# Vision tower on one Trainium2 core: quantization of q, k and v in four passes inside the scale chain, and embedding chunks in one transfer each

## The reference

```python
def fq_act(x, bits=8):                        # one scale for the whole tensor
    mn, mx = jnp.min(x), jnp.max(x)
    qmax = 2.0 ** bits - 1.0
    scale = jnp.maximum((mx - mn) / qmax, 1e-08)
    zero = jnp.round(-mn / scale)
    q = jnp.clip(ste_round(x / scale) + zero, 0.0, qmax)
    return ((q - zero) * scale, scale)
...
qkv = jnp.einsum('bnc,oc->bno', x, fq_weight(w_qkv)) + b_qkv
qkv, _ = fq_act(qkv)                          # first quantization, all three
q, _ = fq_act(qkv[:, :, :C])                  # second quantization, each its own
k, _ = fq_act(qkv[:, :, C:2 * C])
v, _ = fq_act(qkv[:, :, 2 * C:])
...
attn, kv_scale = fq_act(q @ k^T / 4)          # 12 heads of 16 features
out = int_softmax(attn, kv_scale) @ v
```

## Time and profile before

| | us |
|---|---|
| median of 3 runs | 379.75 |
| lowest, highest | 379.64, 383.16 |
| the profiled execution | 379.25 |
| its span in the profile | 377.4 |
| busy: PE, DVE, ACT, POOL | 291.3, 268.6, 203.1, 23.6 |

### The profile page before, as it was taken

One profiled execution on the slowest core, in us unless ns is written; L12 is line 12 of the kernel. 1 busy time (PEld: TensorE's weight loads), 2 busy tenths in 40 slices (PEclk: granted clock), 3 DMA queues, 4 the chain that ended last, 5 costly groups with the idle time before them and its releaser, 6 DMA issues.

```text
span 377.4 us, 5949 instructions
## 1 busy us (share of the span) xinstructions
PE 291.3 (77%) x2232; PEld 266.6 (71%) x2232; DVE 268.6 (71%) x714; ACT 203.1 (54%) x486; POOL 23.6 (6%) x46
## 2 busy tenths in 40 slices
PE   5789979989999999999881042079631598999991
PEld 4577968889999999999771022058420588999991
DVE  1069173888888888798668997975368648888851
ACT  0034546677777777877271467570010667777750
POOL 8010000000000000000000005800000000000000
PEclk9999996999999999999996555569555579999997
DMA  7960400253153132000000000000500013543401
GB/s 235 261 267 1 148 0 4 85 176 125 50 177 116 61 146 72 29 1 2 0 3 0 0 1 2 0 0 2 195 0 1 0 24 114 162 160 126 113 0 43
DMA packets 11548, 27.36 MB, mean 72 GB/s; under 512 B 1496, under 2 KB 3144, under 8 KB 11520
## 3 DMA queue, kind: packets, MB, share of 16 engines
q1 hardware_dynamic: 10944, 26.03, 21.2%
q0 software_dynamic: 576, 0.96, 1.0%
HBM read 26.54 MB, written 0.45 MB: 72 GB/s over the span
## 4 chain that ended last, share of the span: by engine, by line
PE 62%; DVE 22%; ACT 7%; DMA 3%; issue 2%; SPq 2%; DVEq 0%; ACTq 0%
PE bank L585 26%; PE bank L647 9%; PE bank L569 7%; PE bank L632 4%; PE bank L630 4%; DMA embed_area<-w_tok_dram 3%; PE bank L847 2%; DVE embed_area L1510 1%; PE bank L552 1%; PE bank L832 1%; ACT hid_hi L982 1%; DVE bn L1187 1%; PE bank L844 1%; DVE stat_q L1395 1%; PE bank L857 1%
## 5 line engine op out<-in xcount | busy, mean ns | idle before, releaser
L585 PE MATMUL bank<-hid_hi,pj_parts 128*128 128x260 f32 x288 | 76.2, 286 | 1.7 <-DVE hid_lo L1282 1.7
L982 ACT ACTIVATE hid_hi<-hidden_area 128x260 fp32r<-128x260 f32 x144 | 55.9, 422 | 38.8 <-DVE hidden_area L1277 37.6
L1282 DVE TENSOR_TENSOR hid_lo<-hidden_area,hid_hi 128x260 fp32r<-128x260 f32 x144 | 56.6, 427 | 9.9 <-ACT hid_hi L982 0.3
L585 PEld LDWEIGHTS bank<-hid_hi,pj_parts 128*128 128x128 f32 x288 | 54.1, 188 | 2.5 <-DVE hid_lo L1282 2.0
L975 ACT ACTIVATE hidden_area<-bank 128x260 f32<-128x260 f32 x144 | 49.1, 377 | 6.9 <-PE bank L632 6.1
L585 PE MATMUL bank<-xt_hi,fc_hi 128*128 128x260 f32 x144 | 42.8, 297 | 1.3 <-ACT hidden_area L973 1.3
L632 PE MATMUL bank<-xt_lo,fc_lo 128*128 128x260 f32 x144 | 42.2, 293 | 0.0
L585 PE MATMUL bank<-xt_lo,fc_hi 128*128 128x260 f32 x144 | 41.5, 288 | 0.0
L630 PE MATMUL bank<-xt_lo,fc_hi 128*128 128x260 f32 x144 | 41.5, 288 | 0.0
L585 PE MATMUL bank<-xt_hi,fc_lo 128*128 128x260 f32 x144 | 41.3, 287 | 0.0
L647 PE MATMUL bank<-hid_hi,pj_parts 128*128 128x260 f32 x144 | 40.8, 283 | 0.0
(11 more groups left out here) (297 smaller groups left out, 559.3 us busy)
## 6 DMA issues: line engine op xcount, KB each, us to landing
raw_area<-fc_dram SPq DMA_DIRECT2D x8, 768.0 KB, 4.3
raw_area<-pj_dram SPq DMA_DIRECT2D x8, 576.0 KB, 5.4
xn<-comb_dram SPq DMA_DIRECT2D x12, 260.0 KB, 3.3
raw_area<-fc_dram SPq DMA_DIRECT2D x6, 512.0 KB, 4.0
hidden_area<-comb_dram SPq DMA_DIRECT2D x9, 260.0 KB, 3.3
raw_area<-pj_dram SPq DMA_DIRECT2D x6, 384.0 KB, 4.4
embed_area<-patches_dram SPq DMA_DIRECT2D x8, 256.0 KB, 4.7
embed_area<-w_tok_dram SPq DMA_DIRECT2D x8, 96.0 KB, 7.6
```

What stands on the lines that cost most here:

```text
L585: mm = pe.matmul(out, lhs[a], rhs[b], start=start and n == 0, stop=stop and n == 2, skip_group_check=True)
L982: act.activation(hid_hi[:, x % 3, tok], hid_w[:, x % 2, tok], ACT.Copy).then_inc(hid_hi_ready[y], 1)
L1282: dve.tensor_tensor(hid_lo[:, x % 3, tok], hid_w[:, x % 2, tok], hid_hi[:, x % 3, tok].bitcast(F32), ALU.subtract).then_inc(hid_lo_ready[y ...
```

## The change

1. `patches` and `w_tok` become one tensor `embed_in` (in DRAM too), and each of the eight chunks is one transfer of 128 rows of 2816 bytes. PE waits for 16 in place of 32.
2. POOL waits for the last embedding chunk before it issues `wq_raw`; everything behind it on POOL's queue waits as well.
3. The two quantizations of q and of k are each two passes in place of three and a share of a joint one: (x * scale + MAGIC), then (x - MAGIC, min bound). The lower bound is left out, and so are the second lower bound `s2_lo` and `ext_q`. The passes of the first quantization are issued between the small instructions of the scale chain, as soon as `s1_inv` is known. v: ACT does scale and MAGIC of the first quantization after the new semaphore `s1_ready`, DVE clips, ACT multiplies by `ratio`, and DVE (behind `k_heads`) adds MAGIC and clips into `qkv_int`.
4. Two of the six `k_heads` copies (heads 4 and 5) are made by ACT after `k_int_ready`; PE waits for both sets.
5. On PE the wait for all nine groups of scores now stands ahead of `turn_v` in place of behind it.

```diff
-        patches = embed_area.take(128, [TOKK, B * PATCH])
-        w_tok = embed_area.take(128, [TOKK, D])
+        embed_in = embed_area.take(128, [TOKK, B * PATCH + D])
+        patches, w_tok = embed_in[:, :, 0:B * PATCH], embed_in[:, :, B * PATCH:]
...
+        K_HEADS_ACT = (4, 5)
...
             for k in range(TOKK):
-                sp.dma_start(patches[:, k, :], t["patches"][k]).then_inc(tok_in[k], 16)
-                sp.dma_start(w_tok[:, k, :], t["w_tok"][k]).then_inc(tok_in[k], 16)
+                sp.dma_start(embed_in[:, k, :], t["embed_in"][k]).then_inc(tok_in[k], 16)
...
             pool.dma_start(fold[:], t["fold"]).then_inc(consts_in, 16)
+            pool.wait_ge(tok_in[TOKK - 1], 16)
             pool.dma_start(wq_raw[:, 0:6, :], t["w_qkv"]).then_inc(wq_in, 16)
...
             for k in range(TOKK):
-                pe.wait_ge(tok_in[k], 32)
+                pe.wait_ge(tok_in[k], 16)
...
-            pe.wait_ge(k_heads_ready, 1)
+            pe.wait_ge(k_heads_ready, HC - len(K_HEADS_ACT))
+            pe.wait_ge(k_heads_act, len(K_HEADS_ACT))
...
+            pe.wait_ge(sc_ready, 9)
             turn_v()
-            pe.wait_ge(sc_ready, 9)
             statistics(1, stat_s[:], 2, 128)
...
             v = qkv[:, 4:6]
+            act.wait_ge(s1_ready, 1)
+            act.activation(v, v, ACT.Copy, scale=colp("s1_inv", DC)).then_inc(v_act, 1)
+            act.wait_ge(v_act, 1)
+            act.activation(v, v, ACT.Copy, bias=MAGIC).then_inc(v_act, 1)
+            act.wait_ge(v_dve, 1)
             act.wait_ge(s2_ready, 1)
-            act.activation(v, v, ACT.Copy, scale=colp("s1_inv", DC)).then_inc(v_act, 1)
-            act.wait_ge(v_dve, 1)
-            act.activation(v, v, ACT.Copy, bias=MAGIC).then_inc(v_act, 1)
-            act.wait_ge(v_act, 2)
-            act.activation(v, v, ACT.Copy, bias=-MAGIC).then_inc(v_act, 1)
-            act.wait_ge(v_act, 3)
             act.activation(v, v, ACT.Copy, scale=colp("ratio", DC, 2)).then_inc(v_act, 1)
+            act.wait_ge(k_int_ready, 1)
+            for head in K_HEADS_ACT:
+                act.activation(k_heads[:, :, :, head, :], qkv_int[:, 2:4], ACT.Copy,
+                               scale=head_mask[:, head:head + 1]).then_inc(k_heads_act, 1)
...
-            act.wait_ge(v_dve, 2)
-            act.activation(v, v, ACT.Copy, bias=MAGIC).then_inc(v_act, 1)
-            act.wait_ge(v_act, 5)
-            act.activation(qkv_int[:, 4:6], v, ACT.Copy, bias=-MAGIC).then_inc(v_int_ready, 1)
...
             scale_of("s1", col("gmax"), col("gneg"))
-            zero_of("s1", col("gneg"), col("s1_inv"))
...
+            def scaled(x, inv):
+                return step(dve.tensor_scalar(x, x, inv, MAGIC, ALU.mult, ALU.add))
+
+            def clipped(out, x, top):
+                return dve.tensor_scalar(out, x, MAGIC, top, ALU.subtract, ALU.min)
+
+            dve.tensor_scalar(col("s1_z"), col("gneg"), col("s1_inv"), MAGIC, ALU.mult, ALU.add).then_inc(s1_ready, 1)
+            exts = step(dve.tensor_scalar(ext_t[:], ext[:], col("s1_inv"), MAGIC, ALU.mult, ALU.add))
+            q_scaled = scaled(qq, colp("s1_inv", DC))
+            dve.wait_ge(s1_ready, 1)
+            step(dve.tensor_scalar(col("s1_hi"), col("s1_z"), -1.0, MAGIC + QMAX, ALU.mult, ALU.add))
+            step(dve.tensor_scalar(col("s1_lo"), col("s1_z"), MAGIC + QMAX, None, ALU.subtract))
+            tops = step(dve.tensor_scalar(col("s1_step"), col("s1"), 1.0 / QMAX, None, ALU.mult))
+            k_scaled = scaled(kk, colp("s1_inv", DC))
+            after(tops)
+            step(dve.tensor_scalar(ext_c[:, 0:3], ext_t[:, 0:3], MAGIC, col("s1_hi"), ALU.subtract, ALU.min))
+            exts = step(dve.tensor_scalar(ext_c[:, 3:6], ext_t[:, 3:6], MAGIC, col("s1_lo"), ALU.subtract, ALU.max))
+            q_clipped = step(clipped(qq, qq, colp("s1_hi", DC)))
+            after(exts)
+            ranges = step(dve.tensor_tensor(s2, ext_c[:, 0:3], ext_c[:, 3:6], ALU.add))
+            after(k_scaled)
+            k_clipped = step(clipped(kk, kk, colp("s1_hi", DC)))
+            after(ranges)
+            scales = step(dve.tensor_scalar(s2, s2, col("s1_step"), SMIN, ALU.mult, ALU.max))
+            dve.wait_ge(v_act, 2)
+            clipped(v, v, colp("s1_hi", DC)).then_inc(v_dve, 1)
+            after(scales)
             then(dve.reciprocal(s2i, s2))
...
+            dve.tensor_scalar(col("ratio"), s2i, col("s1"), None, ALU.mult).then_inc(s2_ready, 1)
             dve.wait_ge(s2_ready, 1)
...
+            zeros_at = step(dve.tensor_tensor(col("s2_z"), ext_c[:, 3:6], col("ratio"), ALU.mult))
+            q_scaled = scaled(qq, colp("ratio", DC, 0))
+            after(zeros_at)
+            zeros_at = step(dve.tensor_scalar(col("s2_z"), col("s2_z"), MAGIC, None, ALU.add))
+            k_scaled = scaled(kk, colp("ratio", DC, 1))
+            after(zeros_at)
+            then(dve.tensor_scalar(col("s2_hi"), col("s2_z"), -1.0, MAGIC + QMAX, ALU.mult, ALU.add))
+            q_int = step(clipped(qkv_int[:, 0:2], qq, colp("s2_hi", DC, 0)))
+            after(k_scaled)
+            clipped(qkv_int[:, 2:4], kk, colp("s2_hi", DC, 1)).then_inc(k_int_ready, 1)
+            after(q_int)
...
             for head in range(HC):
...
+                if head not in K_HEADS_ACT:
+                    dve.tensor_scalar(k_heads[:, :, :, head, :], qkv_int[:, 2:4], head_mask[:, head:head + 1], None,
+                                      ALU.mult).then_inc(k_heads_ready, 1)
+            dve.wait_ge(v_act, 3)
+            added = step(dve.tensor_scalar(v, v, MAGIC, None, ALU.add))
+            after(added)
+            clipped(qkv_int[:, 4:6], v, colp("s2_hi", DC, 2)).then_inc(v_int_ready, 1)
```

More of the change, by code:

```diff
@@ L202, in build @@
         ext_c = sb("ext_c", [128, 6])
-        ext_q = sb("ext_q", [128, 6])
         c = sb("consts", [128, 80])
@@ L216, in colp @@
             return c[0:p, at + i:at + i + 1]
-        for name in ("s1", "s1_inv", "s1_z", "s1_lo", "s1_hi", "gmax", "gneg", "qk", "alpha", "sa", "sa_inv", "sa_z", "sa_lo",
+        for name in ("s1", "s1_inv", "s1_z", "s1_lo", "s1_hi", "s1_step", "gmax", "gneg", "qk", "alpha", "sa", "sa_inv", "sa_z", "sa_lo",
                      "sa_hi", "x0", "neg_x0", "neg_inv_x0", "neg_x0_30", "quot_bias", "half_b", "sq_bias", "half_b2", "poly_c", "so", "so_inv", "so_z", "so_lo", "so_hi", "alpha_o", "omax",
@@ L293, in build @@
         stat_b = sem("stat_b")
+        s1_ready = sem("s1_ready")
         s2_ready = sem("s2_ready")
+        k_int_ready = sem("k_int_ready")
+        k_heads_act = sem("k_heads_act")
         v_act = sem("v_act")
@@ L1311, in statistics, with step, after @@
                 return PB[7][:, 0:n]
+            def step(ins):
+                steps[0] += 1
+                ins.then_inc(dve_done, 1)
+                return steps[0]
+            def after(n):
+                dve.wait_ge(dve_done, n)
             def scale_of(name, top, negmin, factor=None):
@@ L1414, in _ @@
-            then(dve.tensor_tensor(s2, ext_q[:, 0:3], ext_q[:, 3:6], ALU.subtract))
-            then(dve.tensor_scalar(s2, s2, 1.0 / QMAX, SMIN, ALU.mult, ALU.max))
-            then(dve.reciprocal(s2i, s2))
-            settle(dve.tensor_scalar(col("ratio"), s2i, col("s1"), None, ALU.mult))
-            then(dve.tensor_tensor(col("s2_z"), ext_q[:, 3:6], s2i, ALU.mult))
-            then(dve.tensor_scalar(col("s2_z"), col("s2_z"), -1.0, MAGIC, ALU.mult, ALU.add))
-            then(dve.tensor_scalar(col("s2_lo"), col("s2_z"), MAGIC, -1.0, ALU.subtract, ALU.mult))
@@ L1421, in _ @@
-            dve.tensor_scalar(col("s2_hi"), col("s2_z"), -1.0, MAGIC + QMAX, ALU.mult, ALU.add).then_inc(s2_ready, 1)
-            dve.wait_ge(s2_ready, 1)
-            z = qkv[:, 0:4]
-            then(dve.tensor_scalar(z, z, colp("s1_inv", DC), colp("s1_lo", DC), ALU.mult, ALU.max))
-            then(dve.tensor_scalar(z, z, colp("s1_hi", DC), MAGIC, ALU.min, ALU.add))
-            v = qkv[:, 4:6]
-            dve.wait_ge(v_act, 1)
-            dve.tensor_scalar(v, v, colp("s1_lo", DC), colp("s1_hi", DC), ALU.max, ALU.min).then_inc(v_dve, 1)
@@ L1432, in _ @@
-            for part in range(2):
-                z = qkv[:, 2 * part:2 * part + 2]
-                settle(dve.tensor_scalar(z, z, MAGIC, colp("ratio", DC, part), ALU.subtract, ALU.mult))
-            dve.wait_ge(dve_done, steps[0])
-            for part in range(2):
-                z = qkv[:, 2 * part:2 * part + 2]
-                settle(dve.tensor_scalar(z, z, colp("s2_lo", DC, part), colp("s2_hi", DC, part), ALU.max, ALU.min))
-            dve.wait_ge(dve_done, steps[0])
-            then(dve.tensor_scalar(qkv_int[:, 0:4], qkv[:, 0:4], MAGIC, MAGIC, ALU.add, ALU.subtract))
+            qq, kk, v = (qkv[:, 2 * part:2 * part + 2] for part in range(3))
@@ L1449, in _ @@
             last.then_inc(q_cls_ready, 1)
+            dve.wait_ge(k_int_ready, 1)
             for head in range(HC):
```

(15 more changed lines are left out.)

4 lines of the change are left out of this document (removed).

## The result

| | us |
|---|---|
| median before, 4 runs | 379.69 (379.31 to 383.16) |
| median after, 4 runs | 373.97 (372.01 to 376.04) |
| ratio after to before | 0.9859, 95% interval 0.9811 to 0.9907 |
| predicted | 372.1, range 368.5 to 376.0 |
| the profiled execution of after, its span | 375.34, 373.3 |

A forecast was written before the change was run, and what follows sets the result against it. The prediction took transfers to bound the embedding and DVE the stretch from 204.8 to 228.7 us. Gains of 4.4 + 3.25 = 7.65 us took the median of 379.75 to 372.1, range 368.5 to 376.0.

The forecast's parts named there:

- Embedding, forecast 4.4: Embedding at the start: with faster transfers PE ends its matmuls at 15.9 in place of 20.31 us, 4.4 us gained.
- The bounds: Embedding gain: 2.6 us if only POOL's bytes go out of the way, 5.2 if the first chunk runs at the later pace.
- PE's floor: Embedding matmuls without any wait: 2.93 us for the first chunk plus seven at 1.30, ending at 15.6 us.
- The last chunk: Embedding transfers: the last chunk lands at about 13.8 us and not at 19.02.
- rival A: Embedding transfers: 2816-byte rows cost what two rows did, so 2.6 us gained in place of 4.4, 373.9 us; chance 0.12.
- Behind POOL's wait, forecast nothing: Attention weights `wq_raw` and later loads on POOL's queue: issued later, there by 22.6 us, needed at 23.5; no cost.
- rival C: POOL's wait delays `wq_raw`: costs from a slip of 4 us, at 7 us it costs 3, 375.1 us; chance 0.04.
- Chain, passes and heads, forecast 3.25: Scale chain, quantization passes and head copies on DVE: statistics matmul moves from 228.30 to 225.05 us, 3.25 us gained.
- Rival B: DVE's passes don't pack, or ACT's copies exceed 1.2 us each: 1.4 us gained in place of 3.25, 373.9 us; chance 0.12.
- POOL in the softmax, forecast 0: Softmax's first steps: POOL's mask products leave them, powers of two may block DVE instead; taken as 0, range -0.6 to +1.1 us.
- rival D: Softmax: POOL's powers of two now block DVE, 1.1 us lost, 373.2 us; chance 0.05.
- Rival E: PE's low-clock stretch before the long expert stretch grows: gain gone at 15.3 us more, 384 us at 24 more; chance 0.04.

The follow-up runs named there:

- e1_again: The changed kernel, nothing edited, in six more executions: 372.24 us, ratio 0.9791 to the kernel before.
- e5_no_pool_wait: The changed kernel without POOL's wait for the last embedding chunk, single transfers kept: 376.20 us, ratio 0.9926 to the kernel before.
- e6_two_transfers: The changed kernel with two transfers for each embedding chunk again, POOL's wait kept: 374.07 us, ratio 0.9843 to the kernel before.
- e4_fill: The changed kernel with more filling matmuls on zeros around attention 0: 375.64 us, ratio 0.9867 to the kernel before.
- e11_after_beside: The changed kernel a third time, nothing edited, beside other runs on one chip: 372.42 us, ratio 0.9818 to the kernel before.
- e12_products_beside: The changed kernel with POOL's mask products moved behind its powers of two, beside the unedited changed kernel: 372.88 us, ratio 0.9780 to the kernel before.
- e13_before_again: The kernel before, nothing edited, profiled once more: 379.39 us, ratio 0.9982.
- e10_warm: The changed kernel with nine filling matmuls on zeros ahead of the first embedding chunk: 371.53 us, ratio 0.9792 to the kernel before.

## Why the prediction was right, and which of its terms were off

The time of 373.97 lies 1.9 from the forecast of 372.1, and in its range. The two further medians of the same file are 372.24 and 372.42. That these come within 0.3 of the forecast is partly luck: the embedding's gain was put too high and the chain's too low, and the kernel before, from whose 379.75 the forecast was counted, had medians of 380.91 and 381.32 beside them.

**Embedding, forecast 4.4.** The first layer norm's transposes start 3.75 us earlier in the first pair of profiles (26.02 to 22.27). Over all profiles it is less: kernels with the old embedding start them at 26.02, 25.16 and 24.52, those with the new one at 22.20 to 22.95 in eight and 24.15 in one, medians 25.16 and 22.44, so 2.7. The bounds were 2.6 and 5.2. The term was mis-sized in three places. PE's floor: I took the slow pace for a matter of the first chunk. In the kernel before the second chunk came only at 7.33, when the clock was already up; in the changed one PE starts it at 6.5, and 9 to 19 matmuls ran slowly, as the clock rose earlier or later. So the embedding took 13.29 us and not 12.03 in e1_again. The last chunk: it landed at 15.27 and not at 13.8, since POOL's 0.23 MB cost 30.6 engine-us and not 14; SP's share was right to 1 in 175. And the end before: 20.31 was read off a line with six of the chunk's eight matmuls, it was 20.64.

**Its two causes.** The split was wrong as an argument: rival A took the row size as a term beside POOL's 0.73 MB. Less the quantization's 3.6, the medians at the higher mean clock leave 1.5 us lost with single transfers alone (e5_no_pool_wait), 0.4 gained with the wait alone (e6_two_transfers), and 2.4 to 3.0 gained with both. Five to eight executions each, on different chips, don't fix the sizes; that POOL's wait is needed, both the timeline and twelve executions of e5_no_pool_wait show.

**Behind POOL's wait, forecast nothing.** Right, with less room. The weights landed 10.1 us after issue in place of 8.3, at 26.2 and not 22.6. DVE waited 2.01 us and not 0, which the prediction had named as a sign of being wrong, and 1.41 us of slack were left. That is the way of rival C, stopped short of its price.

**Chain, passes and heads, forecast 3.25.** 3.66 measured, in all ten profiles with the new passes and ACT's copies (20.03 to 20.06 where it was 23.70). The packing is a little better than forecast. ACT's copies took 1.12 each, not 1.16, so they don't hold PE. They are worth 0.79; 0.83 was forecast. Rival B is out.

**POOL in the softmax, forecast 0.** 0.2 lost. The blocking moved as rival D says, but not to the powers of two: to the mask products, which I had expected to leave this stretch. They did leave the steps where they had been, and came to lie on the scale chain of the scores, with the scaling of the last chunk behind them, 1.27 us lost; and 1.06 came back where they no longer are.

**Rival E, the clock.** It was placed in the wrong stretch: I looked at the low stretch ahead of the experts, and it appeared in attention 0, at 41 us. In 14 profiled executions the mean clock and this stretch go together: the four with 0.844 to 0.854 have it (after, e4_fill, e11_after_beside, e12_products_beside), the ten with 0.856 to 0.864 don't. It costs 3.5 us by the first expert matmul (59.66 against 56.15), which is what separates 375.34 from 371.2 to 373.8. Two of four executions in the first measurement were of this kind by their mean clock, none of e1_again's six; that is why the first median lies 1.6 to 1.7 above the two later ones. The kernel before has executions at a low mean clock too (7 of 11, 11 of 17 and 11 of 17 at 0.854 and less in the three sets), but only 3 of 12 in e13_before_again, and no profile caught one, so that theirs are low at the same place is not shown. In the profiles the low stretch is seen in four of nine kernels with the new embedding and in none of the five others; that the earlier start makes it likelier is therefore not excluded. What is shown is that it is not a fixed price of the change.

**The clean size.** Among executions at a mean clock of 0.856 and more, beside the same chip's kernel before, by medians: 378.80 - 372.24 = 6.6 (e1_again, six against four) and 377.91 - 371.90 = 6.0 (e11_after_beside, four against six). By terms: 2.7 to 3.75, plus 3.66, less 0.2, is 6.2 to 7.2. So the forecast of 7.65 was 0.5 to 1.6 us too high, all of it in the embedding.

## What to carry to other kernels

When transfers bound a stage, work out the engine's own floor with its slow start included before adding up what faster transfers bring: here PE became the bound with 12.6 to 13.7 us of its own, and how long its slow start lasted differed between executions. A window that prints the full clock is to be checked against the distance of equal matmuls. Larger rows paid here only once the other queue's bulk transfers were out of the stage, and those could wait only since what they feed had several microseconds of slack. Small instructions can be hidden between long passes at 0.07 us each, but look where the helper engine's work ends up in time when the chain in front of it gets shorter.

## What the runs showed of the hardware that was not expected

- PE's first embedding matmuls start 0.32 us apart and the later ones 0.16. The change comes where the trace's clock record begins, at 6.53 to 11.69 us by the execution, so 8 to 22 matmuls start slowly; ahead of the record the windows print a granted clock of 1.00. Filling from 1.54 to 3.67 us in e10_warm left the first chunk slow.
- The granted clock fell to 1.2 GHz at 41 us while PE was busy almost without a pause (4.92 of 5 us, then 7.00 of 7), in some executions of a file and not in others; filling ahead of it did not prevent it (e4_fill).
- POOL's work stretches DVE instructions on 1 to 50 columns by as much as 0.58 us (0.31 to 0.89), though neither engine handles much data there. On one column those with two inputs grew, those with one did not.
- Two edits of the same transfers bring nothing or a loss (e5_no_pool_wait) and about 0.4 us (e6_two_transfers) alone, and 2.4 to 3.0 together.
